# One core, attention and mixture of experts: sends, expert places, second norms and the last low part are put elsewhere

## The reference

```python
x = x + _layernorm(_L0_attn_ref(_layernorm(x), ...))   # 16 heads of 64, rotary q and k, softmax over all 1024 keys
x = x + _layernorm(_L0_ffn_ref(_layernorm(x), ...))    # router, best 2 of 8 experts of 128 x 256 (SiLU), weighted sum

def _layernorm(x, axis=-1, eps=1e-05):
    m = jnp.mean(x, axis=axis, keepdims=True)
    v = jnp.var(x, axis=axis, keepdims=True)
    return (x - m) / jnp.sqrt(v + eps)
```

## Time and profile before

| what | value |
|---|---|
| runs | 1489.63, 1485.62, 1489.52 us |
| median | 1489.52 us |
| profiled execution, its own time | 1500.58 us |
| its span, first to last instruction | 1498.6 us, 45273 instructions |
| TensorE busy | 1404.8 us, 94% |
| VectorE busy | 1215.5 us, 81% |
| ScalarE busy | 1036.8 us, 69% |
| GpSimd busy | 1154.2 us, 77% |
| sends (L2035) | 48, mean 1301 ns |
| low parts on GpSimd (L2013) | 299, mean 2183 ns |
| low parts on VectorE (L1580) | 213, mean 1685 ns |

### The profile page before, as it was taken

The page is one execution under the profiler, slowest core; times in us unless marked ns, Lnnn a source line. Parts: engine busy times, 40 slices in busy tenths (PEclk is TensorE's granted clock), DMA queues, the critical chain, the costliest instruction groups (busy, mean ns, idle before and its releaser), DMA issues. The chain is left out here.

```text
span 1498.6 us, 45273 instructions
## 1 busy us (share of the span) xinstructions
PE 1404.8 (94%) x17868; PEld 930.3 (62%) x17868; DVE 1215.5 (81%) x2717; ACT 1036.8 (69%) x2010; POOL 1154.2 (77%) x667
## 2 busy tenths in 40 slices
PE   4899999999999999999999999999999999899985
PEld 1366666666666656666666656666666566599764
DVE  7788888888788898888889899888888997765456
ACT  2677777778777877778777767777777676534334
POOL 5588887978787878988787978898879888543464
PEclk8799999999999999999999999999999999999997
DMA  5444444633233324333333323333332252143121
GB/s 169 117 114 142 142 142 123 179 111 97 63 90 84 79 72 108 81 83 81 90 82 94 83 68 97 81 83 79 79 89 61 69 182 62 46 131 90 45 57 55
DMA packets 104081, 142.31 MB, mean 95 GB/s; under 512 B 16960, under 2 KB 51520, under 8 KB 103488
## 3 DMA queue, kind: packets, MB, share of 16 engines
q1 hardware_dynamic: 100800, 133.13, 32.6%
q0 software_dynamic: 3072, 6.30, 1.4%
HBM read 20.49 MB, written 24.38 MB: 30 GB/s over the span
## 5 line engine op out<-in xcount | busy, mean ns | idle before, releaser
L1250 ACT ACTIVATE probs<-psum 128x512 f32<-128x512 f32 x1024 | 614.5, 603 | 251.8 <-PE psum L966 250.9
L2013 POOL TENSOR_TENSOR probs_lo<-probs 128x1024 f16<-128x1024 f32 x299 | 651.3, 2183 | 154.7 <-ACT probs L1250 151.0
L985 PE MATMUL psum<-cv,probs 128*128 128x66 f16 x4096 | 476.3, 193 | 7.8 <-DVE probs_lo L1580 4.8
L987 PE MATMUL psum<-cv,probs 128*128 128x64 f16 x4096 | 475.9, 193 | 0.0
L989 PE MATMUL psum<-cv,probs_lo 128*128 128x66 f16 x4096 | 474.7, 192 | 0.0
L1544 DVE CUSTOM_DVE_ANT_0 scan_out<-psum,ahead 128x512 f16<-128x512 f32 x512 | 346.9, 686 | 131.5 <-PE psum L858 120.0
L987 PEld LDWEIGHTS psum<-cv,probs 128*128 128x128 bf16 x4096 | 380.4, 97 | 110.2 <-issue 2.3
L985 PEld LDWEIGHTS psum<-cv,probs 128*128 128x128 bf16 x4096 | 385.4, 97 | 68.7 <-DVE probs_lo L1580 5.3
L964 PE MATMUL psum<-q_both,k_twice 128*128 128x512 f16 x1024 | 388.4, 379 | 3.5 <-ACT probs L1250 3.2
L966 PE MATMUL psum<-q_max,k_ones 65*128 65x512 f16 x1024 | 390.6, 381 | 0.0
L989 PEld LDWEIGHTS psum<-cv,probs_lo 128*128 128x128 f16 x4096 | 380.0, 98 | 0.0
(11 more groups left out here) (221 smaller groups left out, 1812.0 us busy)
## 6 DMA issues: line engine op xcount, KB each, us to landing
t_swapped<-t_sin SPq DMA_DIRECT2D x248, 128.0 KB, 2.0
k_twice<-qk_hi SPq DMA_DIRECT2D x128, 128.0 KB
slots<-oacc SPq DMA_DIRECT2D x25, 512.0 KB, 3.1
q_lone<-qk_hi SPq DMA_DIRECT2D x64, 128.0 KB, 2.3
q_both<-qk_hi SPq DMA_DIRECT2D x64, 128.0 KB
q_both<-qk_lo SPq DMA_DIRECT2D x64, 128.0 KB
q_max<-qk_hi SPq DMA_DIRECT2D x64, 128.0 KB
k_ones<-qk_lo SPq DMA_DIRECT2D x64, 128.0 KB
```

What stands on the lines that cost most here:

```text
L985: pe.matmul(acc, high[:, q * P:(q + 1) * P, 1], v[:, 0:VLO], start=opens, stop=False, skip_group_check=True)
L987: pe.matmul(acc[:, 0:DH], high[:, q * P:(q + 1) * P, 1], v[:, VLO:VW], start=False, stop=False, skip_group_check=True)
L1250: act.activation(probs[s % 4][:, i, :], score_ps[tile % SCORE_BANKS], ACT.Exp, scale=SCALE).then_inc(probs_done, 1)
L2013: pool.tensor_tensor(probs_lo[s % 4][:].rearrange("p a n -> p (a n)"), p, p.bitcast(BF16).rearrange("p (n two) -> p n two", two=2)[:, :, 1 ...
```

## The change

Four edits, each in a table or in one function:

1. `SEND_AT`: two sends in each of stretches 14 to 29 (steps 5 and 15), where before stretches 16, 24 and 25 had none and 19 and 27 had one. Eight sends leave stretches 30 and 31. In stretch 31 the last is in step 9 instead of 14. Since `SENDING` also sets `LATE_DVE_STEPS`, VectorE makes the low part of step 14 in stretches 16, 24 and 25 too.
2. `PLACE_AT`: `place()` is cut into six parts, four in stretch 30 (steps 1, 5, 9, 13) and two in stretch 31 (steps 3 and 7).
3. `NORM_AT`: z is made by eight ScalarE instructions of 128 x 128, one in each of steps 4 to 11 of place 3, `z = inverse * x + z_shift`. VectorE makes `z_shift` right behind the inverse, and ScalarE waits for it ahead of the first. The four GpSimd instructions stay for the fourth batch alone.
4. `LATE_DVE_STEPS[31]` gets step 15: the very last low part moves from GpSimd to VectorE.

```diff
-SENDING = (14, 15, 17, 18, 19, 20, 21, 22, 23, 26, 27, 28, 29)
-LATE_DVE_STEPS = {**{g: DVE_STEPS + (14,) for g in SENDING}, GROUPS - 2: (1, 3, 5, 7, 9, 11, 13, 15), GROUPS - 1: (0, 1, 2, 4, 5, 6, 8, 9, 10, 12, 13, 14)}
+SENDING = range(14, 30)
+LATE_DVE_STEPS = {**{g: DVE_STEPS + (14,) for g in SENDING}, GROUPS - 2: (1, 3, 5, 7, 9, 11, 13, 15), GROUPS - 1: (0, 1, 2, 4, 5, 6, 8, 9, 10, 12, 13, 14, 15)}
...
-NORM_AT = ((3, 5), (3, 7), (3, 9), (3, 11))
+NORM_AT = tuple((3, 4 + t) for t in range(TILES))
...
-RANK_AT, PLACE_AT = (5, 10), (7, 10)
+RANK_AT = (5, 10)
+PLACE_AT = ((6, 1), (6, 5), (6, 9), (6, 13), (7, 3), (7, 7))
...
-SEND_AT = [(g, s) for g in SENDING for s in ((15,) if g in (19, 27) else (5, 15))]
-SEND_AT += [(g, s) for g in (30, 31) for s in range(STEPS) if s % 4 < 3]
+SEND_AT = [(g, s) for g in SENDING for s in (5, 15)]
+SEND_AT += [(GROUPS - 2, s) for s in (0, 1, 2, 4, 6, 8, 10, 12)]
+SEND_AT += [(LAST, s) for s in (0, 1, 2, 3, 5, 6, 7, 9)]
...
+            def normalise_input(n, t):
+                if t == 0:
+                    act.wait_ge(z_shifted, n + 1)
+                last = act.activation(z_sb[:, t, :], x_sb[:, t, :], ACT.Identity, scale=ln_inv1[:, t:t + 1], bias=z_shift[:, t:t + 1])
+                if t % HALF_TILES == HALF_TILES - 1:
+                    last.then_inc(z_done, 1)
...
+                if k == 1:
+                    dve.wait_ge(inv_done[k], n + 1)
+                    dve.scalar_tensor_tensor(out=z_shift[:], in0=ln_mv1[:, :, 0], scalar=-1.0, in1=ln_inv1[:],
+                                             op0=ALU.mult, op1=ALU.mult).then_inc(z_shifted, 1)
...
-                if epoch and (r, s) in NORM_AT:
-                    normalise_input(epoch - 1, *divmod(NORM_AT.index((r, s)), 2))
```

More of the change, by code:

```diff
@@ L384, in program @@
         ln_inv1 = sb("ln_inv1", [P, TILES])
+        z_shift = sb("z_shift", [P, TILES])
         x_shift = [sb(f"x_shift{b}", [P, TILES]) for b in range(B)]
@@ L1294, in beside @@
                         deviations(1, n)
+                    if (r, s) in NORM_AT:
+                        normalise_input(n, NORM_AT.index((r, s)))
                     if (r, s) in Z_TURNS:
@@ L1728, in _, with place @@
             place_steps = sem("place_steps")
-            def place():
+            def place(part):
                 def step(ins, k):
@@ L1786, in beside @@
                         take_ranks(n)
-                    if (r, s) == PLACE_AT and n == EARLY - 1:
-                        place()
+                    if (r, s) in PLACE_AT and n == EARLY - 1:
+                        place(PLACE_AT.index((r, s)))
                 if b < B:
@@ L2018, in over_rows, with normalise_input @@
                 return t.unsqueeze(2).to_broadcast([P, HALF_TILES, D])
-            def normalise_input(n, half, part):
+            def normalise_input(half, part):
+                n = EARLY
                 tiles = slice(half * HALF_TILES, (half + 1) * HALF_TILES)
@@ L2167, in _ @@
                 for part in range(2):
-                    normalise_input(EARLY, half, part)
+                    normalise_input(half, part)
             finish_tokens(EARLY - 1)
```

48 lines of the change are left out of this document (25 added, 23 removed).

## The result

The changed kernel ran in 1476.8 us (median of 5), the kernel before in 1489.5 beside it (median of 5, which spread over 10 us). The ratio that the measurement gives, with its 95% interval, is 0.9939 (0.9922 to 0.9955), or 9.1 us less; the two medians by themselves stand 12.8 us apart (0.9914), outside that interval, so the gain is about 9 us, known to within a few us. The forecast was faster, 1482.3 us, in a range from 1475.5 to 1487.5. The sign is right, and the range holds the time, near its lower end.

A forecast was written before the change was run, and what follows sets the result against it. TensorE, busy 1404.8 of 1498.6 us, was taken as the bound, so time is won only in its waits or low clock. Stretch 31 -6.0 and norms -1.2 make -7.2 us: 1489.5 to 1482.3 us, range 1475.5 to 1487.5.

The forecast's parts named there:

- Places out of step 10: Stretch 31: with `place` gone from between the low parts of steps 9 and 10, TensorE's 4.4 us stall goes.
- The clock's term: Stretch 31: without the stall the clock stays at 1.00, giving back 2.3 of 4.63 us at half clock.
- So the 0.4 stays and 0.5 is added: Stretch 31: VectorE's existing 0.4 us lateness ahead of `place` remains, and the part in step 7 adds 0.5 us.
- The part of the places in step 7, +0.5: Stretch 31: two fills of 0.17 us and their waits cost 0.5 us; bounds for both parts there 0 and 1.0.
- last low part, -0.5 and +0.7: End of stretch 31: on VectorE the last wait of 0.5 us goes, but VectorE's added work gives back 0.7 us.
- were not waited for: After stretch 31: the first units' loads come earlier and TensorE had not waited for them, so no term was counted.
- Stretch 30, 0 forecast: Four parts of `place`, 2.9 us of VectorE's work, fit into 7.7 free us: 0, bounds -1 and +3.8 us.
- The rival of blocked parts: Stretch 30: `place` parts stand behind GpSimd's low parts; 3.8 us come back, total -3.4, 1486.1 us; chance 0.09.
- Norms, -0.4 in each of three: Stretches 11, 19, 27: 1.0 us of waits goes, 0.6 is paid for ScalarE's wait for `z_shift`; -1.2 us in all.
- Sends, 0: Eight sends moved to stretches 16, 19, 24, 25, 27 cost nothing; bounds 0 and 2.0 us a send.
- the sends starve VectorE: Rival: gapless send and low part on GpSimd leave VectorE nothing; 2.0 us per moved send, 1498.3 us; chance 0.07.

The follow-up runs named there:

- e4: The changed kernel again, unchanged, for a second profile: 1477.6 us against 1487.1 for the kernel before, ratio 0.9943.
- e2: The kernel before with the norms' edit alone (second norms of three batches on ScalarE, `z_shift` on VectorE): ratio 0.9978 to the kernel before.
- e1: The kernel before with the new table of sends alone; norms, places and last low part as before: ratio 1.0075 to the kernel before.
- e8: The kernel before with the new sends and the norms on ScalarE; `place()` in step 10 and the last low part on GpSimd as before: ratio 0.9982.
- e10: The changed kernel with GpSimd's low parts of steps 3 and 7 of stretch 31 on VectorE too: ratio 0.9945 to the kernel before.
- e3: The kernel before with `place()` in six parts and the last low part on VectorE; sends and norms as before: ratio 0.9993 to the kernel before.
- e6: The changed kernel with stretch 31's sends of steps 6, 7, 9 in 8, 9, 10 and `base_rows` behind `lg` in stretch 12: ratio 0.9943 to the kernel before.
- e7: The changed kernel with ScalarE's norms one step later in stretches 11, 19 and 27: ratio 0.9937 to the kernel before.
- e12: The changed kernel with stretch 31's GpSimd low parts (steps 3, 7) on VectorE and stretch 24's step 5 send moved to stretch 31, step 10: ratio 0.9932.
- e5: The kernel before again, unchanged, for a second profile; it fell on another chip, where its median was 1507.4 us.

## Why the prediction was right, and where it was not

The sum was -7.2 us, the ratios give -8.5 and -9.1 (and the medians -9.5 and -12.8). The stretches that the change touches (those shown in the table) give -8.2 in e4, and -2.3 in the first profile, with the 5.5 us of stretch 24. That the sum comes so close is luck in part: stretch 31 gave 2.3 to 2.4 us less than forecast, and the norms and stretch 30 gave about 2 and 1.3 us more.

*Places out of step 10: -4.4 and -2.3 for the clock.* The wait ahead of step 10 went as worked out. The clock's term failed: "I expect the clock to stay at 1.00 then". Another stall of 2.1 us stood ahead of step 6, and the clock was down for 3.45 us behind it instead of 4.63. Stretch 31 won 3.6 us, not 6.0. The step that failed is "So the 0.4 stays and 0.5 is added", the turn that VectorE got at step 6 in the trace, taken over into the changed kernel. There VectorE lost it, as in every other kernel with a send directly ahead of that low part of GpSimd, e2 with no edit in the stretch among them. With the places left in step 10 (e1 and e8) the two stalls are 2.0 us for step 6 and 2.1 for step 10, and stretch 31 is as long as before (-0.1). So there the time lost at step 6 was saved at step 10. Only with GpSimd's two low parts on VectorE as well (e10) did stretch 31 win nearly the 6.0 us forecast (5.7), with the clock at 1.00.

*The part of the places in step 7, +0.5; last low part, -0.5 and +0.7.* The last wait went, and TensorE doesn't stand for the last values at all, so the 0.7 was not paid. The part in step 7 stands behind the stall, at 1287.45, not ahead of it. These two were not measured by themselves.

*The first units "were not waited for".* This held only because the sends were moved too. With the sends as before (e3) 2.5 us of TensorE's standing and a slower clock behind it ate most of the gain. That the two edits need each other here was not in the prediction.

*Stretch 30, 0 forecast.* It was -1.0 to -1.3 in all kernels with the places there, and -0.9 with the sends alone. TensorE stood 0.9 us there (36.19 busy of 37.10) and is now busy throughout. The rival of blocked parts is out.

*Norms, -0.4 in each of three.* Too small: the three stretches are 1.0 to 1.2 us shorter each in e2, whose timed runs say the same (-3.3 in all), and 1.1 to 1.3 each in the changed kernel. Both sides of the working were off. The gain is 2.0 to 2.1 us, not 1.0 (both scan waits went, not the first piece alone), and ScalarE's wait costs 0.7 to 0.9 and not 0.6. In the changed kernel 1.2 us came back in stretch 12 behind `base_rows`, which the prediction didn't look for.

*Sends, 0.* This was the term with the wrong reasoning. The stretches that I read it from, 17 and 25, have no norms. The rival "the sends starve VectorE" names the mechanism, and it is real: 6.7 and 5.9 us for one send each in e1. In the change it is taken out of 19 and 27 by the norms' move (e8). It is left in stretch 24, where it struck in three of the six profiles that have a send there in step 5 and the norms on ScalarE (the first, e6 and e7, not e4, e8 and e10). The Trainium skill, "SBUF — State Buffer", section "Who interferes with whom", gives the pair of ports to one engine for a whole instruction. That agrees with the 1.21 us that became 3.33. But a low part of 8.20 us is more than one instruction of GpSimd: VectorE's low part lost every turn until GpSimd paused. By the rule as I used it (one low part of 1.9 us per collision) the worst case was far too small.

What goes with a long low part in stretch 24 is when GpSimd's second rope addition gets its load. In the profiles with the changed norms and a send there, GpSimd waited 2.06, 1.84, 1.73 and 1.74 us for it where the low part took 5.6 to 5.8 us, and 0.39, 0.30, 0.15 and 0.16 where it took 2.6 or less. VectorE wrote the data at the same time in all (from 9.0 to 9.2 us into the stretch, for 0.68 us). In the late ones SyncE issued the second half's load 0.1 to 0.6 us later, and it took 3.2 to 3.6 us to land, against 2.1 to 2.3 in the others. Why it is late in some executions stays open, as does the spread of the untouched stretches.

## What to carry to other kernels

Where VectorE and GpSimd both work from SBUF, look in GpSimd's timeline for chains without a gap, not at its busy share. What starts on VectorE inside a chain can be kept until the chain ends, and a send of 1 us can close the last gap. A share of the work given to GpSimd can cost VectorE more in blocking (1.7 us) than the work itself (1.14). A turn that VectorE got in one trace may be lost in the next kernel though nothing near it was edited (1.21 us against 3.33), so price both outcomes. Test the parts of a change alone and in pairs: here they add up to +0.46% and the whole is -0.57%. Before two profiles are compared to a few us, take one of them a second time, on the same chip.

## What the runs showed of the hardware

- A low part of VectorE, 1.21 us by itself, can lose many turns in a row: it took 8.20 us beside six instructions of GpSimd without a gap and 5.84 beside four. A gap of 0.02 to 0.03 us between a send and a low part of GpSimd was enough for VectorE's turn in the two profiles of the kernel before (1.21 us at step 6 of stretch 31) and not in eight others at the same place (3.33). Behind a gap of 0.41 us (e12) no such wait built up.
- Instructions of VectorE with an input in PSUM (scan, `rot`, `t_sin`: 0.67 to 0.69 us) keep their time beside GpSimd's low parts. `base_rows`, a `tensor_scalar` with one input in SBUF, doesn't. It took 0.21 to 1.86 us, by where in GpSimd's row of low parts it began, and unlike the low parts above it always got its turn when the one beside it ended, in seven of the profiles with the next one following without a gap.
- The same kernel took 1507.4 us on one chip and 1486 to 1489 on the others. Nearly all of it, 20 us, is behind the attention (196.5 to 197.4 us against 176 to 177 without e3), where by the last two windows under e5 TensorE is busy 11.3 us longer (at a clock of 0.91 for 0.95) and idle 8.2 us longer, in waits whose releaser the profile doesn't show (6.0 us at one line) and in two for `y_got` (4.8 us, the longer 3.4). The cause was not tried.
